# GpSimd multiplies every third block of 32 rows by the scale in the output stage; VectorE only adds PSUM there

## The reference

```python
h = jnp.maximum(_layernorm(x, axis=-1), 0.0)
z = jnp.concatenate([h[source], h[target], edge_attrs], axis=-1)
m = jax.nn.sigmoid(z @ W_f + b_f) * jax.nn.softplus(z @ W_s + b_s)
message = jax.ops.segment_sum(m, source, num_segments=100000)
mean = jnp.mean(message, axis=0)
var = jnp.mean((message - mean) ** 2, axis=0)
normed = (message - mean) * jax.lax.rsqrt(var + BN_EPS) * gamma + beta
return x + h + normed
```

## Time and profile before

| what | value |
|---|---|
| median of three runs | 1109.26 us |
| profiled execution, its own time | 1113.39 us |
| its span in the trace | 1111.7 us |
| DVE busy over the span | 708.8 us (64%) |
| PE busy over the span | 611.0 us (55%) |
| POOL busy over the span | 689.8 us (62%), none of it after about 907 us |
| multiply L1097, 33 instructions | 57.1 us, 1730 ns mean |
| `m_buf` loads, 38 | 21.6 us median to landing |

### The profile page before, as it was taken

The page is one execution under the profiler, slowest core; times in us unless marked ns, Lnnn a source line. Parts: engine busy times, 40 slices in busy tenths (PEclk is TensorE's granted clock), DMA queues, the critical chain, the costliest instruction groups (busy, mean ns, idle before and its releaser), DMA issues. The chain is left out here.

```text
span 1111.7 us, 11420 instructions
## 1 busy us (share of the span) xinstructions
PE 611.0 (55%) x2864; PEld 414.8 (37%) x2864; DVE 708.8 (64%) x1427; ACT 473.5 (43%) x1118; POOL 689.8 (62%) x596
## 2 busy tenths in 40 slices
PE   0305645453645573645664645654635636699978
PEld 0203433342424362424542424532424535543322
DVE  3102776565756695657675666855757865599878
ACT  0103646364544574544663555563645724500000
POOL 6773787878787788787878788778786530000000
PEclk9755776766767666767666667767667759999989
DMA  8955334334343444333333233333232349969999
GB/s 329 402 175 171 66 87 97 81 86 81 83 83 82 102 103 79 66 64 56 53 65 62 47 65 43 67 63 61 48 64 37 66 132 400 401 215 422 426 427 377
DMA packets 78297, 162.13 MB, mean 146 GB/s; under 512 B 39755, under 2 KB 46251, under 8 KB 69675
## 3 DMA queue, kind: packets, MB, share of 16 engines
q1 hardware_dynamic: 27947, 98.94, 24.4%
q0 software_dynamic: 40768, 19.31, 15.7%
q10 hardware_dynamic: 9536, 43.43, 9.7%
HBM read 93.87 MB, written 67.75 MB: 145 GB/s over the span
## 5 line engine op out<-in xcount | busy, mean ns | idle before, releaser
L385 POOL DMA_INDIRECT xg<-in_x_dram,ids x392 | 378.3, 965 | 121.2 <-issue 115.3
L398 POOL DMA_INDIRECT msgs_dram<-comb,target x196 | 310.4, 1584 | 91.1 <-issue 57.9
L697 ACT ACTIVATE comb<-bank_c 128x256 f32<-128x256 f32 x49 | 18.8, 384 | 351.2 <-remote 320.4
L750 PE MATMUL bank_c<-ident,eas 128*128 128x128 f32 x49 | 21.0, 429 | 261.7 <-ACT comb L697 240.4
L562 DVE TENSOR_TENSOR msg<-gate,soft 128x256 f32<-128x256 f32 x49 | 21.1, 431 | 224.9 <-ACT gate L660 148.0
L792 PE MATMUL bank_c<-msg,same 128*128 128x64 f32 x980 | 138.3, 303 | 10.7 <-ACT same L690 5.7
L792 PEld LDWEIGHTS bank_c<-msg,same 128*128 128x128 f32 x980 | 134.7, 221 | 11.8 <-ACT same L690 6.1
L502 DVE SCALAR_TENSOR_TENSOR not_later<-ps_src,own,upto 128x128 f32<-128x128 f32 x196 | 67.2, 346 | 80.3 <-remote 80.3
L750 PEld LDWEIGHTS bank_c<-ident,eas 128*128 128x128 f32 x49 | 8.9, 181 | 271.0 <-issue 270.6
L781 PEld LDWEIGHTS ps_v<-w_z,z_t 128*128 128x128 f32 x392 | 91.9, 322 | 48.4 <-issue 48.4
L690 ACT ACTIVATE same<-same,one_col 128x512 f32<-128x512 f32 x196 | 107.6, 550 | 1.6
(11 more groups left out here) (106 smaller groups left out, 974.5 us busy)
## 6 DMA issues: line engine op xcount, KB each, us to landing
m_buf<-msgs_dram SPq DMA_DIRECT2D x38, 1024.0 KB, 21.6
xn<-in_x_dram SPq DMA_DIRECT2D x48, 512.0 KB
out_dram<-m_buf ACTq DMA_DIRECT2D x20, 1024.0 KB, 10.8
msgs_dram<-zeros SPq DMA_DIRECT2D x11, 1536.0 KB
y_spill_dram<-y_kept ACTq DMA_DIRECT2D x19, 512.0 KB
y_kept<-y_spill_dram SPq DMA_DIRECT2D x9, 1024.0 KB, 16.5
msgs_dram<-zeros ACTq DMA_DIRECT2D x5, 1536.0 KB
xg<-in_x_dram,ids POOLq DMA_INDIRECT x392
```

What stands on the lines that cost most here:

```text
L385: pool.indirect_dma_start(xg[:, n % G_SLOTS, 2 * j + c, :], None, x, bass.IndirectOffsetOnAxis(ap=ids[:, c, n * TILES + j:n * TILES + j + ...
L398: pool.indirect_dma_start(msgs, bass.IndirectOffsetOnAxis(ap=target[:, n % UNROLL, j:j + 1], axis=0), comb[:, n % UNROLL, j, :], None, com ...
```

## The change

A constant `POOL_EVERY = 3` is added. `pool_parts` holds all parts of the positions 5, 8, 11, 14, 17, 20 and 23, so six whole blocks (one of them of 29 rows) and four parts of 8 rows. GpSimd waits for the scale once, then multiplies these in this order, each as soon as its load is there. VectorE leaves out their multiply, waits for GpSimd's semaphore in its place and adds PSUM as before.

```diff
+        pool_parts = [k for k, (i, _, _) in enumerate(y_parts) if i % POOL_EVERY == POOL_EVERY - 1 and i > POOL_EVERY]
...
+        @block.gpsimd
+        def _(pool):
+            pool.wait_ge(scale_ready, 1)
+            for k in pool_parts:
+                i, r, n = y_parts[k]
+                m = m_buf[:, buf_of(i), r:r + n, :]
+                pool.wait_ge(m_loaded[buf_of(i)], 16 * loads_of(i))
+                pool.tensor_tensor(m, m, scale[:, :].unsqueeze(1).to_broadcast([P, n, F]), ALU.mult
+                                   ).then_inc(pool_scaled, 1)
...
-            dve.tensor_tensor(scale[:, :], var[:, :], gam[:, :], ALU.mult).then_inc(chain, 1)
+            dve.tensor_tensor(scale[:, :], var[:, :], gam[:, :], ALU.mult).then_inc(scale_ready, 1)
...
             for k, (i, r, n) in enumerate(y_parts):
                 m = m_buf[:, buf_of(i), r:r + n, :]
-                dve.wait_ge(m_loaded[buf_of(i)], 16 * loads_of(i))
-                dve.tensor_tensor(m, m, scale[:, :].unsqueeze(1).to_broadcast([P, n, F]), ALU.mult).then_inc(scaled, 1)
-                dve.wait_ge(scaled, k + 1)
+                if k not in pool_parts:
+                    dve.wait_ge(m_loaded[buf_of(i)], 16 * loads_of(i))
+                    dve.tensor_tensor(m, m, scale[:, :].unsqueeze(1).to_broadcast([P, n, F]), ALU.mult
+                                      ).then_inc(scaled, 1)
+                    dve.wait_ge(scaled, len([j for j in range(k + 1) if j not in pool_parts]))
+                else:
+                    dve.wait_ge(pool_scaled, pool_parts.index(k) + 1)
                 dve.wait_ge(y_summed, k + 1)
                 dve.tensor_tensor(m, m, ps_y(k), ALU.add).then_inc(added, 1)
```

More of the change, by code:

```diff
@@ L74 @@
 Y_AHEAD = 2
+POOL_EVERY = 3
 SPLIT = 3
@@ L860, in stage_two @@
         scaled = sem("scaled")
+        scale_ready = sem("scale_ready")
+        pool_scaled = sem("pool_scaled")
         y_taken = sem("y_taken")
@@ L1068, in _ @@
             dve.wait_ge(affine_loaded, 32)
-            dve.tensor_tensor(scale[:, :], var[:, :], gam[:, :], ALU.mult).then_inc(chain, 1)
+            dve.tensor_tensor(scale[:, :], var[:, :], gam[:, :], ALU.mult).then_inc(scale_ready, 1)
+            dve.wait_ge(scale_ready, 1)
+            dve.tensor_tensor(mean2[:, :], mean[:, :], scale[:, :], ALU.mult).then_inc(chain, 1)
             dve.wait_ge(chain, 3)
-            dve.tensor_tensor(mean2[:, :], mean[:, :], scale[:, :], ALU.mult).then_inc(chain, 1)
-            dve.wait_ge(chain, 4)
             dve.tensor_tensor(shift[:, :], bet[:, :], mean2[:, :], ALU.subtract).then_inc(shift_ready, 1)
@@ L1078, in _ @@
                 dve.tensor_copy(part[:, k, :], shift[:, :] if k == 0 else left[:, k, :]).then_inc(chain, 1)
-                dve.wait_ge(chain, 5 + 2 * k)
+                dve.wait_ge(chain, 4 + 2 * k)
                 if k < SPLIT - 1:
@@ L1082, in _ @@
                                       ALU.subtract).then_inc(chain, 1)
-                    dve.wait_ge(chain, 6 + 2 * k)
+                    dve.wait_ge(chain, 5 + 2 * k)
             for k in range(SPLIT):
```

## The result

The changed kernel takes 1121.74 us (median of four runs, 1120.03 to 1123.46) against 1109.23 us: 12.5 us slower, a ratio of 1.0111 with a 95% interval of 1.0098 to 1.0124, so 10.9 to 13.8 us. The forecast was 1119.5 us, 10.2 us slower. In an experiment further down (the probe with multiplies), one of four executions took 1776.24 us at a granted clock of 0.362; it stands in none of the figures.

What follows compares the result with a forecast made beforehand. Bytes bound the output stage once stores start, and compute its 35.2 us tail after position 17 lands. The terms 8.1 + 2.1 + 0 - 1.0 + 1.0 = +10.2 us on 1109.26 gave 1119.5 us, range 1109 to 1125.

Steps and rivals of the forecast that it cites:

- Start, 8.1 us: After the scale, VectorE's small instructions take turns with GpSimd's multiplies; first multiply at about 990.2, not 982.10: 8.1 us late.
- Price on GpSimd, 4.4 us: A GpSimd multiply of 2048 elements, each input costing a read: 4.4 us, against VectorE's 2.29 us.
- Positions 5 and 8, 0: VectorE skips 2.29 + 2.1 us there; TensorE, then the full DMA engines, take that: 0.
- Positions 11 and 14, 0: In the stretch of full DMA engines, a store 2 us later leaves the bandwidth to loads: 0.
- Position 17, 2.1 us: At the load VectorE waits for, the add comes 4.4 us after the landing and not 2.29: +2.1 us.
- TensorE's clock at the start, +1: The 8 us of waiting puts TensorE's first parts at the lower clock: 0 to +3 us, taken as +1 us.
- Position 20, 0: GpSimd's multiply saves VectorE 2.29 us but may block position 19's or 21's: between -2.3 and +4.4, taken as 0.
- Position 23, -1.0 us: Near the end, four VectorE multiplies of 0.69 go; about one and a half is won: -1.0 us.
- rival 1: Both engines multiply side by side with no conflict: -2 to +1.5 us, so 1107 to 1111 us; chance 0.20.
- once only at the start (2): VectorE's chain gets through between GpSimd's first and second multiply; start costs 4.4, total 6.5: 1115.8 us; chance 0.08.
- the dearer multiply (3): A GpSimd multiply takes 6.0 us; start costs 11.2, position 17 3.7: about +15, 1124.5 us; chance 0.07.
- Slowed but not excluded (4): VectorE's instructions beside GpSimd's take twice as long; start costs 1 to 2 us: 1110 to 1114 us; chance 0.10.

Runs made afterwards that it cites:

- the probe with multiplies: Kernel before, plus four GpSimd multiplies of 128x1024 into a scratch tile nobody reads, once the scale is made: 1094.62 us, ratio 1.0082.
- 5 and 8 alone: Changed kernel, but GpSimd multiplies only positions 5 and 8, VectorE the rest: 1094.88 us, ratio 1.0082 against the kernel before.
- the later start: Changed kernel with all seven positions, but GpSimd's first multiply waits until VectorE has added six parts: 1112.55 us, ratio 1.0022 against the kernel before.
- the two probes: Kernel before plus idle GpSimd work on a scratch tile: four multiplies (1094.62 us, ratio 1.0082) or eight MEMSETs of 128x1024 (1089.44 us, ratio 1.0022).
- TensorE relieved: Kernel before with the seven positions' multiplies left out and TensorE adding shift to one row of each part only: 1109.95 us, ratio 0.9999.
- the free multiplies: Kernel before with the multiplies of the seven positions left out, VectorE only waiting for loads and adding PSUM: 1085.87 us, ratio 1.0000.

## Why the prediction was right

The time of 1121.74 us lies in the range, 2.2 us above the forecast, and the mechanism (turns between the engines, at the start of the stage) is shown by the trace and by four kernels: 5 and 8 alone, the later start, and the two probes.

The forecast of 10.2 us was too low by more than the noise (10.9 to 13.8 us), and the sum is closer than its terms. The trace has 8.3 us up to the landing of position 17 (7.7 against the second trace of before), where I had 9.1 with TensorE's clock, and 2.2 + 0.6 us behind it, where I had 1.1. These two errors point opposite ways, and that they partly cancel is luck.

*Start, 8.1 us.* It measured 8.0 in the trace. The step was right in its cause and off in a detail: I had `left` wait for GpSimd's second multiply, and the CAST ahead of it did, with one SBUF input. I had reckoned with conflicts for two inputs only. The sum didn't change, since one turn was lost either way.

*Price on GpSimd, 4.4 us.* It is 4.50. I had drawn it from instructions of 128 elements and chosen it among 3.1, 4.4 and 6.0 us, so that it came this near was partly luck. The Trainium skill's figure for an add of this size (GPSIMD Engine Reference, Performance versus the Vector engine) is 4497 ns, and the trace agrees for a multiply; with it my sum grows by 0.3 us, and not by 0.4 as I wrote.

*Positions 5 and 8, 0.* Right in size. The reason was half wrong: I named TensorE first and the full DMA engines second, and with TensorE relieved nothing is won either. Once the stores run, it is the bytes.

*Positions 11 and 14, 0.* Right: without 5 and 8 on GpSimd, the landing of position 17 comes 94.8 us after the scale's start, against 94.1 and 94.7 in the two traces of before.

*Position 17, 2.1 us.* Right for the add (2.2). Alone it costs 3.4 us (2.2 to 4.6), so the term may be too small, by an amount that the interval leaves open. TensorE's lower clock behind that add is no shown reason. In after, its matmuls there took 6.63 us, but in the kernel before they took 5.37 in one trace and 3.67 in the other, at the same length of the tail:

```profile
1084.14 6.63 PE L1010 MATMUL ps_all<-y_kept,ident 128*128 128x512 f32 x8 [2.33 <-DVE m_buf L1119]
```

The same place in the first trace of the kernel before:

```profile
1078.10 5.37 PE L1005 MATMUL ps_all<-y_kept,ident 128*128 128x512 f32 x8 [2.73 <-DVE m_buf L1100]
```

*TensorE's clock at the start, +1.* The clock did fall: behind the late `shift_row` four matmuls took 3.78 us, where eight take 3.70, and the granted clock from 985.5 to 991 is 0.50.

```profile
987.41 3.78 PE L1010 MATMUL ps_all<-y_kept,ident 128*128 128x512 f32 x4
```

VectorE's lead of small parts hid it but for 0.93 us of waiting at position 2, and at the landing of position 17 nothing of it is left: 8.3 or 7.7 us late, for 8.0 at the start. The term should have been about 0 here. In the probe with multiplies it was not: VectorE's first multiply was 6.4 us late and the landing of position 17 8.1 to 8.6.

*Position 20, 0.* Its multiply held up position 19's by 5.25 - 2.29 = 3.0 us, and 2.29 were saved: within the bounds given, and close to nothing.

*Position 23, -1.0 us.* This term failed. Position 23 alone on GpSimd brings the last add 0.6 us nearer to the landing of position 17, but the time does not fall (1.2 us slower, 0.2 to 2.2). I had read the last 35 us as compute because VectorE never idles in them. The DMA engines were full there too, to 1104, and an add that comes earlier only waits longer for its store: with the free multiplies VectorE ends 3.6 us ahead of the span's end, with TensorE relieved 4.0, in the kernel before 2.2 to 2.5. Compute and transfers are even in this tail, so that being later costs and being earlier does not pay. In after, GpSimd's four pieces of position 23 also met VectorE's multiplies, which is why they took 8.59 us and not 4.94.

*Rivals.* Side by side without conflict (rival 1) is refuted by `shift` at 4.40 us, once only at the start (2) by the CAST at 3.98, the dearer multiply (3) by 4.50 us. Slowed but not excluded (4) is refuted by rows that end about 0.1 us behind GpSimd's. GpSimd started 0.08 us after the scale was done, and not 0.24, which changed nothing.

## What to carry to other kernels

Before moving half of an elementwise pair to GpSimd, look at which of VectorE's instructions will run beside it: beside a GpSimd multiply, those with two SBUF inputs and copy-like ones (CAST, TENSOR_SCALAR) can wait for a whole GpSimd instruction each, while the adds that read PSUM did not wait. A bad place for it is beside a chain of small dependent instructions on which everything waits; hold GpSimd back with a semaphore until the chain is through (here 10 of 12.5 us). And where the DMA engines are at 1.01 share, try first what the saving would bring if it were free, by leaving the work out: here nothing.

## What the runs showed of the hardware

A CAST of 128x64 from float32 to bf16, with one SBUF input, took 3.98 us beside a GpSimd multiply, and 0.5 to 0.7 us beside MEMSETs of 1.0 us each (eight in 8.02 us), where it takes 0.20 alone; a subtraction with two SBUF inputs kept its 0.23 us beside the MEMSETs and took 4.40 beside the multiply. GpSimd pays as well: two multiplies of 8.58 us took 12.56 us beside VectorE's large ones. GpSimd's multiply of 2048 float32 takes 4.50 us with a row of 64, repeated 32 times, as one input.
